# Edge gathers of a graph layer: an explicit bound on the row numbers of the indirect DMAs

## The chip, the cores and the metric

The kernel runs on one core of one Trainium2 chip. The metric is the device time in microseconds. Three runs of the kernel before took 1586.07, 1587.04 and 1588.51 us; the median is 1587.04 us.

## What is computed

A graph layer over 6250 nodes with 512 features and 106250 directed edges, sorted by their target, is followed by a mixture of 16 experts. Cut to what matters:

```python
def _L0_gnn_ref(x, src, dst, W_self, b_self, W_neigh, gamma, beta, alpha):
    deg = jax.ops.segment_sum(jnp.ones_like(src, dtype=x.dtype), dst, num_segments=N)
    inv_deg = 1.0 / jnp.maximum(deg, 1.0)
    agg = jax.ops.segment_sum(x[src], dst, num_segments=N)
    neigh = agg * inv_deg[:, None]
    h = x @ W_self + b_self + neigh @ W_neigh
    ...  # layer norm over features, gamma, beta, leaky slope alpha
    return h + x

x = x + _L0_gnn_ref(_layernorm(x), src, dst, ...)
x = x + _L0_ffn_ref(_layernorm(x)[None], gate_weight, w1, w2)[0]
```

The change touches `x[src]`, the fetch of one row per edge. `src` holds numbers from 0 to 6249.

## The kernel before

The work goes in three parts, one after another.

Projection. The rows of x are normalised in 49 tiles of 128 nodes and multiplied by W_neigh before they are aggregated. The product, split into a high and a low half of type float16, goes to a table in device memory (`table`, 6250 rows of 1024 float16 values, 2048 bytes a row, stored in line 427).

Edge stage. The 106250 edges are cut into 208 groups (`GROUPS`) of 4 times 128 edges (`GT` is 4). For each group GpSimd (POOL) issues four indirect DMAs in line 656; each fetches 128 rows of the table, one per partition, by a column of `idx_all`, into a ring of four group buffers (`GRING`, tile `gath`, printed as work). So there are 832 gathers of 256 KB. From the fifth group on, POOL first reads from a small table how many steps TensorE must have finished before the buffer is free (`value_load` in line 651), waits for that number on `c_step` (line 652) and executes a `nop` (line 653). The places behind the last edge of the last group get source number 0 (line 572 clears that part of the list) and target -1, so each number in `idx_all` is a row of the table.

TensorE (PE) takes the rows in 257 steps (`STEPS`): each step waits until its group has landed (`c_g`) and multiplies the rows by a 128 by 128 matrix of zeros and ones that ScalarE (ACT) builds (lines 781 and 787), so that the rows of one target are added up in PSUM (line 1035); line 1038 counts the edges, and its last matmul raises `c_step`. Beside the first 49 steps PE also computes x @ W_self for one tile a step (`side`, whose matmuls are in line 931). VectorE (DVE) finishes a tile of nodes when its last step is done (line 1411 is the first of its instructions). In the last 49 steps PE transposes the finished tiles (line 1052) and computes the gate's logits for them.

Experts. Then DVE and ACT sort the tokens by expert, and POOL gathers the tokens, 128 a time, in 114 indirect DMAs of line 715. PE multiplies them by the experts' weights, the means per expert are formed, and the result is mixed into the output. The gathers of line 715 wait for the list that DVE writes in line 1609.

Waits are written out by hand, each engine runs its program in order, and the only instructions that POOL executes between line 649 and line 658 are those named above.

Of the kernel before, what the change touches and what calls it, by code (L numbers as in the profile page):

```python
# [5 lines left out]
N, D, EXPERTS, FF = 6250, 512, 16, 256  # L6
# [13 lines left out]
GRING = 4  # L20
# [86 lines left out]
def build(nc, x, src, dst, w_self, b_self, w_neigh, gamma, beta, alpha, gate_t, w1_t, w2_t, out):  # L107
# [7 lines left out]
    with ctx:  # L115
# [3 lines left out]
        def sems(name, n):  # L119
            return [sem(f"{name}{i}") for i in range(n)]  # L120
# [68 lines left out]
        def cut(words, start=None):  # L189
            if start is not None:  # L190
                place[0] = start
            a = place[0]
            place[0] += words
            assert place[0] <= WORK, place[0]
            return work[:, a:a + words]
# [13 lines left out]
        idx_all = cut(GROUPS * GT, WORK - TABLES).bitcast(i32)  # L209
# [133 lines left out]
        c_g = sems("c_g", GRING)  # L343
# [225 lines left out]
        def _(pool):  # L569
# [79 lines left out]
            for g in range(GROUPS):  # L649
                if g >= GRING:  # L650
                    at = pool.value_load(finrow[0:1, g - GRING:g - GRING + 1], min_val=HOTS + 1, max_val=HOTS + STEPS)  # L651
                    pool.wait_ge(c_step, at)
                    pool.nop(nofuse=True)
                for w in range(GT):
                    t = GT * g + w
                    pool.indirect_dma_start(  # L656
                        out=gath[:, g % GRING, w, :], out_offset=None, in_=table[:, :],
                        in_offset=bass.IndirectOffsetOnAxis(ap=idx_all[:, t:t + 1], axis=0)).then_inc(c_g[g % GRING], 16)


            pool.wait_ge(d_zero, 16)
# [46 lines left out]
            for k in range(SLOTS):  # L708
                it, b = divmod(k, RING)
                if it:  # L710
# [6 lines left out]
                    in_offset=bass.IndirectOffsetOnAxis(ap=idx2[:, k:k + 1], axis=0)).then_inc(f_g[b], 16)  # L717
# [1001 lines left out]
```

## Time and profile before

| what | value |
|---|---|
| median of three runs | 1587.04 us |
| lowest, highest | 1586.07, 1588.51 us |
| span of the profiled execution | 1584.0 us |
| POOL busy | 986.1 us (62%) |
| gathers of line 656, busy | 793.9 us in 832 instructions |
| PE busy | 1149.7 us (73%) |
| DVE busy | 1079.2 us (68%) |
| ACT busy | 888.5 us (56%) |
| mean granted TensorE clock | 0.914 |

The page comes from one execution. Its span reaches from the first to the last instruction and is 3.0 us below the median of the runs. An instruction of an engine is shown with its busy time and with the idle time ahead of it, together with what ended that idle time; "issue" means that the engine waited for nothing which the profile shows. POOLq stands for POOL's sequencer, which fetches and issues instructions. The landing of a DMA is what releases the engines that wait for its data.

### The profile page before, as it was taken

Reading aid. Unit: us, or ns where it says so; the run is one execution under the profiler, and the core shown is the slowest. Engines: PE = TensorE matmul, PEld = TensorE weight load, DVE = VectorE, ACT = ScalarE, POOL = GpSimd, SP = SyncE. Lnnn points to the kernel's source line nnn. Section 1 sums busy time; section 2 is a strip of 40 time slices with the busy share of each in tenths; the row PEclk is TensorE's granted clock in tenths of the full one; section 3 lists DMA queues with packets and bytes.
Section 4 is the critical chain, followed back from the end, with each engine's and each line's share of the span. In section 5 each row is a group of like instructions: output and inputs, shape, how many; then the busy total and the mean of one; then the engine's idle time right before and its main releaser. Section 6 shows DMA issues by size and latency. Waiting matters only on the chain.

```text
span 1584.0 us, 36317 instructions
## 1 busy us (share of the span) xinstructions
PE 1149.7 (73%) x7603; PEld 615.1 (39%) x7604; DVE 1079.2 (68%) x2597; ACT 888.5 (56%) x1925; POOL 986.1 (62%) x1254
## 2 busy tenths in 40 slices
PE   4999999999655555665556555566667527999986
PEld 2555444444322222222222222224444315766741
DVE  5776236657667675777878778657666895677647
ACT  3565455555645444554444444437666696888850
POOL 5323377676777777777777777777777305676500
PEclk9999999999979898888898998979999958999995
DMA  5545378887888898899988888888887636777659
GB/s 186 162 157 172 125 219 269 260 250 248 273 273 274 260 268 240 256 300 299 298 289 288 295 293 295 265 247 250 248 253 235 226 130 186 243 238 243 201 172 334
DMA packets 140644, 384.92 MB, mean 243 GB/s; under 512 B 22358, under 2 KB 22488, under 8 KB 140524
## 3 DMA queue, kind: packets, MB, share of 16 engines
q0 software_dynamic: 76416, 250.05, 52.5%
q1 hardware_dynamic: 63580, 132.49, 23.3%
q10 hardware_dynamic: 528, 1.05, 0.2%
q8 instruction: 43, 0.70, 0.2%
q14 instruction: 77, 0.63, 0.1%
HBM read 323.78 MB, written 59.72 MB: 242 GB/s over the span
## 4 chain that ended last, share of the span: by engine, by line
PE 39%; POOL 26%; issue 18%; DVE 7%; DMA 6%; POOLq 2%; ACT 2%; DVEq 0%; SPq 0%; ACTq 0%
POOL work L656 25%; PE ps L931 13%; PE ps L1035 10%; PE ps L1127 6%; DMA work<-table,work 4%; PE ps L1138 3%; PE ps L1129 3%; POOLq L651 2%; PE ps L1205 1%; PE ps L979 1%; DMA work<-in_x 1%; DVE slots L1600 1%; ACT slots L846 1%; PE ps L1189 0%; DVE stats L1312 0%
## 5 line engine op out<-in xcount | busy, mean ns | idle before, releaser
L656 POOL DMA_INDIRECT work<-table,work x832 | 793.9, 954 | 284.8 <-issue 238.3
L1035 PE MATMUL ps<-work 128*128 x2056 | 552.9, 418 | 339.2 <-DMA work<-table,work 315.3
L1035 PEld LDWEIGHTS ps<-work 128*128 128x128 f16 x2056 | 212.4, 104 | 572.9 <-issue 421.3
L787 ACT ACTIVATE work<-work,ones 128x512 f16<-128x512 f16 x257 | 183.9, 716 | 300.8 <-PE ps L1038 300.7
L781 ACT ACTIVATE work<-iota_row,work 128x128 f16<-128x128 f32 x1028 | 327.5, 390 | 27.4 <-ACT work L787 23.9
L931 PE MATMUL ps<-wparts,slots 128*128 128x512 f16 x1176 | 271.9, 382 | 4.4 <-DVE work L1333 2.4
L715 POOL DMA_INDIRECT slots<-x_d,betab x114 | 110.4, 968 | 135.8 <-DVE betab L1609 67.3
L1411 DVE TENSOR_SCALAR inv<-ps 128x1 f32 (+2 forms) x49 | 7.7, 158 | 231.2 <-PE ps L1038 226.2
L931 PEld LDWEIGHTS ps<-wparts,slots 128*128 128x128 f16 x1176 | 112.4, 99 | 124.9 <-issue 7.3
L1127 PE MATMUL ps<-work,wparts 128*128 x456 | 155.7, 382 | 0.9 <-issue 0.4
L875 ACT COPY wparts<-ps 128x1024 f16<-128x1024 f16 x114 | 115.3, 1011 | 38.1 <-PE ps L1138 36.9
L1129 PE MATMUL ps<-work,wparts 128*128 x456 | 124.8, 274 | 0.0
L1636 DVE TENSOR_REDUCE work<-ps 128x256 f32<-128x512 f32 x114 | 78.4, 690 | 34.6 <-PE ps L1129 30.6
L1038 PEld LDWEIGHTS ps<-onesh,work 128*128 128x128 f16 x1028 | 66.9, 100 | 71.9 <-issue 19.8
L801 ACT COPY wparts<-ps 128x1024 f16<-128x1024 f16 (+1 forms) x49 | 49.4, 1008 | 79.3 <-PE ps L1052 79.3
L1628 DVE TENSOR_TENSOR slots<-slots,work 128x256 f32 x114 | 62.3, 546 | 35.9 <-issue 21.5
L793 ACT ACTIVATE slots<-ps,wscale 128x512 f32<-128x512 f32 (+1 forms) x49 | 33.6, 686 | 92.6 <-PE ps L931 92.6
L1138 PE MATMUL ps<-identh,slots 128*128 128x128 f16 x912 | 70.4, 221 | 7.2 <-DMA slots<-x_d,betab 7.2
L1138 PEld LDWEIGHTS ps<-identh,slots 128*128 128x128 f16 x912 | 61.0, 99 | 22.3 <-issue 7.4
L733 ACT ACTIVATE work<-work,gb,gs 128x512 f32<-128x512 f32 (+1 forms) x49 | 40.1, 821 | 45.4 <-POOL gb L624 45.3
L1038 PE MATMUL ps<-onesh,work 128*128 128x1 f16 x1028 | 63.5, 165 | 0.0
L869 ACT ACTIVATE work<-work,wscale 128x256 f32<-128x256 f32 x114 | 58.1, 510 | 8.8 <-DVE work L1636 8.1
(284 smaller groups left out, 1506.0 us busy)
## 6 DMA issues: line engine op xcount, KB each, us to landing
work<-in_x SPq DMA_DIRECT2D x96, 256.0 KB, 2.8
work<-in_w_t SPq DMA_DIRECT2D x48, 512.0 KB, 6.7
work<-table,work POOLq DMA_INDIRECT x832
table<-work SPq DMA_DIRECT2D x48, 256.0 KB, 2.0
x_d<-work SPq DMA_DIRECT2D x48, 256.0 KB
x_d<-slots SPq DMA_DIRECT2D x48, 256.0 KB
slots<-x_d SPq DMA_DIRECT2D x48, 256.0 KB
out_x<-slots SPq DMA_DIRECT2D x48, 256.0 KB
```

What stands on the lines that cost most here:

```text
L656: pool.indirect_dma_start(out=gath[:, g % GRING, w, :], out_offset=None, in_=table[:, :], in_offset=bass.IndirectOffsetOnAxis(ap=idx_all[: ...
L715: pool.indirect_dma_start(out=xf[:, b, :], out_offset=None, in_=x2_d[:, :], in_offset=bass.IndirectOffsetOnAxis(ap=idx2[:, k:k + 1], axis= ...
L781: last = act.activation(away[:, par, w, :], iota_row[:, :], ACT.Abs, bias=negd[:, ds(GT * k + w, 1)])
L787: act.activation(hot[:, slot, :, :], away[:, slot % 2, :, :], ACT.Relu, bias=ones[:, 0:1], scale=-1.0).then_inc(c_hot, 1)
L875: act.copy(xft[:, b, :, :, :], chunks16(bank16(6 + n % 2), P)).then_inc(f_xt, 1)
L931: last = pe.matmul(to, left(a, c), right(w, c), start=start and c == 0 and a == 0 and w == 0, stop=c == n - 1 and a == 1)
L1035: pe.matmul(ps[:, ds(bank, 1), :], hot[:, s, w, :], gath_row[:, ds(at + (2 * w + half) * D, D)].unsqueeze(1), start=False, stop=True, skip ...
L1038: last = pe.matmul(ps[:, BANKS:2 * BANKS, 0:1][:, ds(bank, 1), 0], hot[:, s, w, :], onesh[:, :], start=False, stop=True, skip_group_check= ...
L1127: pe.matmul(ps[:, HBANK + b, :].rearrange("p (u a n) -> p u a n", u=1, a=2), xft[:, b, 0, c, :], both, start=c == 0, stop=c == CHUNKS - 1, ...
L1129: last = pe.matmul(ps[:, HBANK + b, FF:2 * FF].unsqueeze(1), xft[:, b, 1, c, :], high, start=False, stop=c == CHUNKS - 1, skip_group_check ...
L1138: last = pe.transpose(bank16(6 + n % 2)[:, j * P:(j + 1) * P], xf[:, b, j * P:(j + 1) * P], identh[:, :])
L1636: dve.tensor_reduce(hid[:, b, :], ps[:, HBANK + b, :].rearrange("p (a n) -> p n a", a=2), X, ALU.add).then_inc(f_pre, 1)
```

## The change

Each of the 832 gathers of the edge stage is given `bounds_check=N - 1`, which is 6249, and `oob_is_err=False`: a row whose number is above the bound is skipped, and nothing is reported. Without the two arguments there is no bound, and `oob_is_err` has its default, True. The gathers of line 715 stay as they are.

```diff
                     t = GT * g + w
                     pool.indirect_dma_start(
                         out=gath[:, g % GRING, w, :], out_offset=None, in_=table[:, :],
-                        in_offset=bass.IndirectOffsetOnAxis(ap=idx_all[:, t:t + 1], axis=0)).then_inc(c_g[g % GRING], 16)
+                        in_offset=bass.IndirectOffsetOnAxis(ap=idx_all[:, t:t + 1], axis=0),
+                        bounds_check=N - 1, oob_is_err=False).then_inc(c_g[g % GRING], 16)
```

The program interface takes the bound as a number or as a register.

## Rows read from the trace of the kernel before

**Rows 1.** Page: span, and the chain that ended last by engine and line.

```profile
span 1584.0 us, 36317 instructions
...
PE 39%; POOL 26%; issue 18%; DVE 7%; DMA 6%; POOLq 2%; ACT 2%; DVEq 0%; SPq 0%; ACTq 0%
```

**Rows 2.** Windows by stage: stretch, length, each engine's busy us, clock, DMA share, GB/s.

```profile
core 0: us, PE busy (x) PEld busy (x) DVE busy (x) ACT busy (x) POOL busy (x), PEclk, DMA share, GB/s
190.60:1246.70 1056.10, 717.74 (x4512) 358.30 (x4511) 721.31 (x1886) 568.41 (x1378) 793.86 (x832) 0.92 0.84 266
```

**Rows 3.** The gathers of line 656: durations, and idle time ahead of them.

```profile
L656 POOL DMA_INDIRECT work<-table,work x832: 942/949/1379, 190.6 to 1245.7; - x167
...
  issue: 238.3, 781
  PE ps L1038: 24.0, 50
```

**Rows 4.** Timeline of POOL, one group of gathers and the next one's first: start, duration, idle time before.

```profile
607.64 0.94 POOL L656 DMA_INDIRECT work<-table,work  x1 [0.30 <-PE ps L1038]
...
611.39 0.96 POOL L656 DMA_INDIRECT work<-table,work  x1 [0.30 <-issue]
612.66 0.95 POOL L656 DMA_INDIRECT work<-table,work  x1 [0.30 <-issue]
```

**Rows 5.** Windows of the edge stage's beginning, middle and end, columns as in rows 2.

```profile
190.60:405.40 214.80, 210.07 (x1136) 97.62 (x1134) 118.16 (x312) 122.15 (x300) 156.08 (x164) 1.00 0.81 253
405.40:1041.00 635.60, 368.44 (x1880) 173.78 (x1881) 465.56 (x1198) 314.24 (x793) 481.50 (x506) 0.87 0.87 278
1041.00:1246.80 205.80, 139.32 (x1499) 86.92 (x1498) 137.69 (x377) 132.13 (x286) 156.28 (x163) 0.96 0.80 245
```

**Rows 6.** Timeline of POOL, gathers that waited over 0.5 us for a buffer.

```profile
292.60 0.95 POOL L656 DMA_INDIRECT work<-table,work  x1 [1.56 <-PE ps L1038]
...
314.68 0.95 POOL L656 DMA_INDIRECT work<-table,work  x1 [2.35 <-PE ps L1038]
...
385.35 0.95 POOL L656 DMA_INDIRECT work<-table,work  x1 [2.34 <-PE ps L1038]
```

**Rows 7.** POOL's sequencer at lines 651 and 653: min, median and max ns.

```profile
L651 POOLq TENSOR_LOAD <-work x204: 283/289/1005, 195.8 to 1229.7; - x102
L651 POOLq FUSED_REGOPS  x204: 147/147/193, 196.3 to 1230.0; - x102
L651 POOLq SEQ_ASSERT  x204: 18/18/32, 196.5 to 1230.2; - x102
L653 POOLq EVENT_SEMAPHORE  x204: 17/17/17, 202.5 to 1236.0; - x102
```

**Rows 8.** The chain of waits about 605 us: start, us, what.

```profile
604.92 0.60 POOLq L651
```

**Rows 9.** Page: all packets; POOL's DMA queue: packets, MB, share of 16 engines.

```profile
DMA packets 140644, 384.92 MB, mean 243 GB/s; under 512 B 22358, under 2 KB 22488, under 8 KB 140524
...
q0 software_dynamic: 76416, 250.05, 52.5%
```

**Rows 10.** The waits: who waited for whom, us in total, times, longest.

```profile
PE ps L1035 <- DMA work<-table,work: 315.3, 166, 5.8
ACT work L787 <- PE ps L1038: 300.7, 138, 7.3
DVE inv L1411 <- PE ps L1038: 226.2, 43, 33.4
```

**Rows 11.** The token gathers of line 715, durations as in rows 3.

```profile
L715 POOL DMA_INDIRECT slots<-x_d,betab x114: 941/948/1192, 1314.0 to 1510.4; - x114
```

**Rows 12.** Groups of POOL: a tensor instruction on four elements a partition.

```profile
L614 POOL TENSOR_TENSOR fix<-guess 128x4 f32<-128x4 f32 x39 | 7.8, 200 | 3.1
```

**Rows 13.** Timeline at the stage's end: the last gathers, and DVE behind PE.

```profile
1240.05 0.16 DVE L1411 TENSOR_SCALAR inv<-ps 128x1 f32<-128x1 f32 x1 [0.77 <-PE ps L1038]
...
1245.73 0.95 POOL L656 DMA_INDIRECT work<-table,work  x1 [0.30 <-issue]
```

## The prediction

> **What bounds the kernel now.** I read the page's chain first. PE has 39% of it, POOL 26%, and 18% is "issue", time in which an engine waited for nothing that the profile shows [rows 1]. Shares of a whole span hide which stage an edit touches, so the windows by stage come next: the gathers of line 656 fill the stretch from 190.6 to 1246.7 us, 1056.1 of the 1584.0 us, and POOL does nothing else there [rows 2]. Then the gathers themselves. Nearly all take 949 ns (median, 942 at least), and the idle time ahead of them is 238.3 us of issue in 781 gaps, which makes 0.305 us a gap, plus 24.0 us for PE in 50 [rows 3]. The timeline shows what that looks like: a gather starts each 1.25 us, with 0.30 us between two, at a group's first gather as at its others [rows 4]. 832 times 1.25 us is 1040 us, all but 16 us of the stage. So the stage runs at the pace of POOL's own work, and the reader should see in rows 4 that the 0.30 us is part of that pace and no wait.
>
> The windows inside the stage correct this in one place. Up to 405.4 us PE is busy for 210.07 of 214.80 us: there it also has the W_self product, and it is PE that sets the pace. After that it is busy for 368.44 of 635.60 and 139.32 of 205.80 us [rows 5]. POOL's real waits say the same: five gathers waited between 1.56 and 2.35 us for a buffer, the first at 292.6 and the last at 385.35 us, 10.3 us together with the usual gap of 0.30 in each, hence 8.8 us of real slack [rows 6]. 164 gathers lie ahead of 405.4 us and 506 and 163 (one of them counted in both) behind it, 668 in all [rows 5]. Downstream everybody waits for them: PE 315.3 us for landings, ACT 300.7 us for PE, DVE 226.2 us for PE [rows 10]. Even at the end DVE's last chain is set off by a PE step, at 1240.05 us, while the last gathers are still issued [rows 13].
>
> **The exchange rate.** It follows that x ns more per gather cost 668x behind 405.4 us, and nothing ahead of it until 164x exceeds 8.8 us, that is until x is 53. So 10 ns are 6.7 us. What a measurement of this kernel can tell from no change is about 0.2%, 3.2 us, and that is 4.8 ns per gather. A gain of x ns would bring the same 668x, until the next limit: the 16 DMA engines are busy for 87% of the middle [rows 5], so at most 13% of 841 us, 109 us.
>
> **The change part by part.** (1) Rows saved. None: each number in the list is a row of the table, since the unused places hold number 0. The bytes and the descriptors stay, so the landings and the 87% stay. Cost 0, and no gain. This has one answer as long as the bound is counted in rows.
>
> (2) Handing over the bound. A number has to reach the instruction as an operand. If a register is set once, it costs nothing; if it is set ahead of each gather, there are 832 more instructions on POOL's sequencer. Rows 7 have the neighbours of such an instruction: 17 to 18 ns for the simplest, 147 ns for a fused register operation. What covers them: in front of each group the sequencer already executes a load, a register operation and an assertion, 289 + 147 + 18 = 454 ns, and then the wait and the nop, and the gap of the group's first gather stays 0.30 us like the others' [rows 4, 7]. The chain shows line 651 at 604.92 us for 0.60 us, and the gather it belongs to starts at 607.64 us [rows 4, 8]: the sequencer is 2.1 us ahead, more than one gather. Four times 147 ns are 588 ns a group, beside 5.01 us in which POOL works off four gathers; the lead would still be made. I take 0. Were the cover gone, because an operand that comes from a register cannot be queued ahead, it would cost 18 to 147 ns per gather: 668 times that is 12 to 98 us, and at the upper end the first 164 gathers add 164 x 0.147 - 8.8 = 15 us, which makes 113 us.
>
> (3) Comparing the row numbers. The queue of these transfers is named software_dynamic [rows 9] and each gather costs POOL 949 ns, so I assume that the comparison is made where POOL writes the descriptors, on its own path. No gather with a bound stands in the trace; the token gathers have none either and take the same, 948 ns [rows 11]. From below: the compare is already there with some bound that lets everything pass, and costs 0; or the default form does a check with its error report that the new form leaves out, a gain. A gain is priced by the cheapest check in the trace, the sequencer's assertion with 18 ns [rows 7]: 668 x 0.018 = 12 us. From above: a separate pass of POOL over 128 numbers, priced by its smallest tensor instructions, 200 ns [rows 12]: 668 x 0.200 = 134 us, and 24 us more from the first stretch. Between them lies a compare and branch inside the loop: a row now costs 949 / 128 = 7.4 ns for reading its number, working out an address and writing the descriptors; a compare at a twentieth to a sixth of that is 0.4 to 1.2 ns a row, 50 to 160 ns a gather, 33 to 120 us (estimates from rows 3). I take 0, because the nearest rows, 832 and 114 gathers of different tables, agree to 1 ns and so look like one fixed piece of work done on all 128 numbers, into which a compare fits without a step of its own; but this is a choice, not a reading, and both ends stay in the range.
>
> (4) Packets. The queue carries 250.05 MB in 76416 packets [rows 9]. 22358 packets of all queues are under 512 B [rows 9]; if 16 of them belong to each of the 946 gathers, 15136 in all, 61280 packets of 4080 bytes remain, two rows each (an estimate from rows 9). A bound might force one row per packet, since a row could be missing. The price would fall on the DMA engines, which have 13% left [rows 5]; q0 uses 52.5% of the span for its 250 MB. I take 0: up to 13% longer transfers are hidden by the issue pace, and beyond that it would show as a DMA share near 1.
>
> Sum against the profiled execution: 1584.0 + 0 + 0 + 0 + 0 = 1584.0 us of span, and 3.0 us around it by the median of the runs: 1587.0 us.
>
> The rows show that writing descriptors is the pace of the stage: 0.95 of each 1.25 us [rows 4]. The Trainium skill, "DMA: Bandwidth & Descriptors", section "Anatomy of one DMA — SWDGE (gpsimd) path", calls descriptor generation "small, variable" and says that the fixed cost of some 2 us is mostly the receipt of the last write. Taken literally this would make any check free, and the time 1587.0 us by another road; the gaps of rows 4 speak against it, for nothing hides behind a landing there. By the rows a check of 50 ns costs 33 us, by the page nothing.
>
> **The rivals.** *The check costs in the descriptor loop* (slower). One mechanism: each of the 128 numbers meets a compare and a branch, the duration of line 656 rises from 949 ns by 5 to 200 ns, and from 4.8 ns on it can be told. For it: POOL's work is on the path, with no slack for 668 gathers. Against it: the sameness of all gathers. At 60 ns: 668 x 0.060 = 40 us, plus 164 x 0.060 - 8.8 = 1 us: 1628 us. Chance 0.34.
>
> *The register is on the path* (slower). The duration stays, the gap of 0.30 us grows by 18 to 147 ns. Against it speaks the lead of 2.1 us [rows 4, 8]. At 18 ns 1599 us, at 147 ns 1700 us. Chance 0.08, nearer to the lower end.
>
> *The default form was the dearer one* (faster). The duration falls, because no error has to be looked for; 18 ns give 1575 us. For it speaks only that something must happen today with a number outside the table. Chance 0.12, of which 0.03 for more than 18 ns.
>
> *The change does not do what it says*: if the bound is compared in another unit than rows, rows are skipped, the DMA share falls and the result lacks rows. The issue pace would hardly move; chance 0.02, and its time would be that of one of the other cases.
>
> *No effect*: chance 0.44, 1587.0 us, own range 1584 to 1590 us.
>
> **How the numbers follow.** The likeliest case gives 1587.0 us. Slower by over 0.2%: 0.34 + 0.08 = 0.42. Faster by over 0.2%: 0.12, and 0.01 of the case of the wrong unit: 0.13. Within 0.2%: 0.45. The range takes in the gain of 18 ns, 1575 us, with a little beyond, 1574; upward it follows the loop's check to 110 ns: 668 x 0.110 = 73 us, plus 164 x 0.110 - 8.8 = 9 us, which is 1670; I take 1668. Left out are about 0.04 below and 0.12 above.
>
> **What would show it.** The median duration of line 656 decides (3), the usual gap of 0.30 us decides (2), the packets of q0 and the DMA share decide (4). If POOL's pace is 1.25 us again, the span must be 1584 within its scatter. If it is not, the five waits of rows 6 should shrink first, and the length behind 405.4 us should grow by 668 times the difference. I am wrong if the pace moves by more than 4.8 ns, or if the span moves while the pace does not.

## The result, and the profile after

The changed kernel took 1623.98 us (median of 4 runs, 1622.89 to 1625.09) against 1587.77 us for the kernel before beside it. The ratio is 1.0224, with a 95% interval from 1.0211 to 1.0238: 2.2% slower. The profiled execution's span grew from 1584.0 to 1621.5 us, by 37.5 us. The forecast of no change was wrong. The time lies in the range, and it came where the first rival had put it: in the gather's own duration. That rival's mechanism, a compare for each of the 128 numbers, is another matter (see the gathers of fewer rows).

The page and the gathers' line after the change. The durations are min, median and max ns, then come first and last start:

```profile
span 1621.5 us, 37149 instructions
...
DMA packets 140651, 384.98 MB, mean 237 GB/s; under 512 B 22358, under 2 KB 22488, under 8 KB 140524
...
q0 software_dynamic: 76416, 250.05, 51.7%
```

```profile
L656 POOLq MOVE  x832: 29/29/35, 190.2 to 1273.4; - x167
L656 POOL DMA_INDIRECT work<-table,work x832: 994/999/1297, 191.0 to 1281.8; - x167
...
  issue: 240.1, 788
  DMA table<-work: 23.2, 1
  PE ps L1039: 14.9, 43
```

Against [rows 3] the median has risen from 949 to 999 ns, and even the shortest gather takes 994 instead of 942. A second line is new: 832 register moves of 29 ns on POOL's sequencer, one ahead of each gather, which are exactly the 832 instructions that the page counts more. POOL's queue carries the packets and MB of [rows 9], to the packet; over all queues there are 7 packets more, all on the queue q14, whose kind the page calls instruction. (Lines below 656 have moved down by one: 1039 here is 1038 before.)

The timeline of POOL, the stretch of [rows 4]:

```profile
606.30 1.00 POOL L656 DMA_INDIRECT work<-table,work  x1 [0.30 <-issue]
607.61 0.99 POOL L656 DMA_INDIRECT work<-table,work  x1 [0.30 <-issue]
608.91 1.00 POOL L656 DMA_INDIRECT work<-table,work  x1 [0.30 <-issue]
610.21 1.00 POOL L656 DMA_INDIRECT work<-table,work  x1 [0.30 <-issue]
```

The gap is 0.30 us as before, the gather is longer, and the pace is 1.30 instead of 1.25 us.

Where the 37.5 us lie: the first gather starts 0.5 us later (191.04 for 190.57). From the first start to the last, the stage takes 1281.82 - 191.04 = 1090.8 us, where it took 1245.73 - 190.57 = 1055.2: 35.6 more. Behind the last start come 339.7 instead of 338.3 us, 1.4 more. The 35.6 us come out of two sums. The gathers are busy for 836.8 instead of 793.9 us, 42.9 more, and the idle time ahead of them, without the first gather's, is 240.1 + 14.9 = 255.0 instead of 262.3 us, 7.3 less. What shrank are the waits for a buffer in the first stretch. Five waits of over 0.5 us stood there, all of over 1.5 us [rows 6]; two of over 0.5 us are left:

```profile
364.80 1.00 POOL L656 DMA_INDIRECT work<-table,work  x1 [1.17 <-PE ps L1039]
...
386.88 1.00 POOL L656 DMA_INDIRECT work<-table,work  x1 [1.25 <-PE ps L1039]
```

The 165th gather, the first behind the stretch in which PE sets the pace, divides the stage. Before (first line) and after (second):

```profile
405.52 0.94 POOL L656 DMA_INDIRECT work<-table,work  x1 [0.44 <-issue]
407.90 1.00 POOL L656 DMA_INDIRECT work<-table,work  x1 [0.30 <-issue]
```

From the first gather to this one it takes 216.9 instead of 214.9 us, 1.9 more, and from this one to the last 873.9 instead of 840.2 us, 33.7 more.

The windows, with the columns of [rows 2], answer to [rows 5]:

```profile
190.60:405.40 214.80, 209.50 (x1130) 97.27 (x1129) 116.68 (x308) 120.55 (x297) 163.19 (x163) 1.00 0.81 249
405.40:1041.00 635.60, 378.55 (x1809) 173.31 (x1808) 449.59 (x1156) 304.30 (x767) 487.81 (x486) 0.82 0.85 268
```

Up to 405.4 us PE is as busy as before and nearly as many gathers start, 163 for 164. In the middle only 486 gathers start where 506 did. The DMA share fell from 0.87 to 0.85, so the DMA engines had less to do and not more. PE's granted clock fell too (0.87 to 0.82) and its matmuls took longer, but it waited for landings 318.2 us in all (315.3 before), and behind 386.88 us no gather waited over 0.5 us for it, so it was not what the stage waited for.

### The profile page after: what moved, and what is told of

Its sections match the earlier page's. It is cut to its first block, busy times and chain, and to the rows that moved or that the text cites. A ratio compares the mean times of both kernels' runs of the same rounds, so it can differ in the third digit from the quotient of the medians.

```text
span 1621.5 us, 37149 instructions
## 1 busy us (share of the span) xinstructions
PE 1184.8 (73%) x7603; PEld 626.2 (39%) x7604; DVE 1078.1 (66%) x2597; ACT 889.0 (55%) x1925; POOL 1028.6 (63%) x1254
## 2 busy tenths in 40 slices
DMA packets 140651, 384.98 MB, mean 237 GB/s; under 512 B 22358, under 2 KB 22488, under 8 KB 140524
## 3 DMA queue, kind: packets, MB, share of 16 engines
q0 software_dynamic: 76416, 250.05, 51.7%
## 4 chain that ended last, share of the span: by engine, by line
PE 40%; issue 25%; POOL 18%; DVE 5%; DMA 4%; POOLq 4%; ACT 2%; DVEq 0%; SPq 0%; ACTq 0%
POOL work L656 17%; PE ps L932 13%; PE ps L1036 12%; PE ps L1128 6%; POOLq L651 3%; DMA work<-table,work 3%; PE ps L1139 3%; PE ps L1130 3%; PE ps L1206 1%; PE ps L980 1%; DMA work<-in_x 1%; POOLq L656 1%; DVE slots L1601 1%; ACT slots L847 1%; PE ps L1039 0%
## 5 line engine op out<-in xcount | busy, mean ns | idle before, releaser
L656 POOL DMA_INDIRECT work<-table,work x832 | 836.8, 1006 | 278.2 <-issue 240.1
L1036 PE MATMUL ps<-work 128*128 x2056 | 585.8, 437 | 340.8 <-DMA work<-table,work 318.2
L1036 PEld LDWEIGHTS ps<-work 128*128 128x128 f16 x2056 | 218.4, 107 | 591.4 <-issue 451.8
L1637 DVE TENSOR_REDUCE work<-ps 128x256 f32<-128x512 f32 x114 | 78.3, 690 | 35.5 <-PE ps L1130 31.4
L1039 PEld LDWEIGHTS ps<-onesh,work 128*128 128x128 f16 x1028 | 69.5, 103 | 79.7 <-issue 33.7
```

The source lines that it names most:

```text
L656: pool.indirect_dma_start(out=gath[:, g % GRING, w, :], out_offset=None, in_=table[:, :], in_offset=bass.IndirectOffsetOnAxis(ap=idx_all[: ...
L1036: pe.matmul(ps[:, ds(bank, 1), :], hot[:, s, w, :], gath_row[:, ds(at + (2 * w + half) * D, D)].unsqueeze(1), start=False, stop=True, skip ...
L1039: last = pe.matmul(ps[:, BANKS:2 * BANKS, 0:1][:, ds(bank, 1), 0], hot[:, s, w, :], onesh[:, :], start=False, stop=True, skip_group_check= ...
L1637: dve.tensor_reduce(hid[:, b, :], ps[:, HBANK + b, :].rearrange("p (a n) -> p n a", a=2), X, ALU.add).then_inc(f_pre, 1)
```

## The experiments

The theory after the result: a bound makes each indirect DMA dearer by 50 ns of POOL's own work, whatever it is told to do with rows beyond it, and this shows in the time where POOL sets the pace and nowhere else. The rivals: the silent skipping is what costs (B); the register move or its hand-over costs (C); and, for the size of the price, that it goes by the rows compared (E) and not by the instruction (D).

**The bound, with an error for rows beyond it**

```diff
-                        bounds_check=N - 1, oob_is_err=False).then_inc(c_g[g % GRING], 16)
+                        bounds_check=N - 1).then_inc(c_g[g % GRING], 16)
```

> The bound stays on all 832 gathers, but a row beyond it is reported (oob_is_err left at True). Theory A, the comparison itself costs: the median of the gathers is 999 ns as in the changed kernel, ratio to the kernel before 1.022. Theory B, skipping without an error is what costs: the median is back near 949 ns and the ratio is 1.000 to 1.003. In between would mean both.

Measured: ratio 1.028, interval 1.0259 to 1.0301, and

```profile
L656 POOL DMA_INDIRECT work<-table,work x832: 1006/1012/1525, 190.6 to 1290.7; - x167
```

B falls: with the error form the price is 63 ns, 13 more than in the silent one, where medians of the same form differ by up to 4 ns from kernel to kernel (946 and 949 without a bound, 998 to 1002 with the silent one). A held in kind, and was low in size. The exchange rate fits: 668 x 0.063 + (164 x 0.063 - 8.8) = 43.6 us, measured 0.028 x 1588.6 = 44.5.

**The silent form, without a bound**

```diff
-                        in_offset=bass.IndirectOffsetOnAxis(ap=idx_all[:, t:t + 1], axis=0)).then_inc(c_g[g % GRING], 16)
+                        in_offset=bass.IndirectOffsetOnAxis(ap=idx_all[:, t:t + 1], axis=0),
+                        oob_is_err=False).then_inc(c_g[g % GRING], 16)
```

(The edit is shown against the kernel before.)

> Only the other argument: oob_is_err=False with no bound. Theory A (the bound costs): 949 ns, ratio 1.000. Theory B (the silent form costs): 999 ns, ratio 1.022. If the default form looked for errors at a price, as my rival of the faster side had it, the median would fall below 949 ns.

Measured: ratio 0.9993, interval 0.9983 to 1.0002, and

```profile
L656 POOL DMA_INDIRECT work<-table,work x832: 940/946/1348, 192.5 to 1247.0; - x167
```

The two arguments taken apart give the split: without a bound, the silent form costs nothing, and the price is the bound's. The 3 ns below [rows 3] are no gain: kernels whose gathers were not touched, or only the first 164 of them, show 946 as well (below). So the default form without a bound pays nothing that could be saved, and my rival of the faster side falls.

**The bound in a register that is set once**

```diff
+            top_row = nc.alloc_register(pool.engine, "top_row")
+            pool.reg_mov(top_row, N - 1)
             for g in range(GROUPS):
...
-                        bounds_check=N - 1, oob_is_err=False).then_inc(c_g[g % GRING], 16)
+                        bounds_check=top_row, oob_is_err=False).then_inc(c_g[g % GRING], 16)
```

> The bound is put into a register once, ahead of the loop, so the 832 register moves of 29 ns on POOL's sequencer are gone and all else is as in the changed kernel. Theory A (the cost sits in the gather's own work, the moves are covered): gathers stay at 999 ns, gaps at 0.30 us, ratio 1.022 like the changed kernel, within 0.2% of it. Theory C (the move or its hand-over costs): 832 times 29 ns, up to 24 us, come back, ratio near 1.007.

Measured: 1622.10 us, ratio 1.0206, interval 1.0189 to 1.0223, beside the changed kernel's 1.0211 to 1.0238. The moves are gone from the sequencer, and the gathers (first fence) and their gaps in the timeline (second) are as they were; line 658 is line 656 here:

```profile
L658 POOL DMA_INDIRECT work<-table,work x832: 996/1002/1281, 191.2 to 1282.0; - x167
```

```profile
600.37 1.00 POOL L658 DMA_INDIRECT work<-table,work  x1 [0.31 <-issue]
601.68 1.00 POOL L658 DMA_INDIRECT work<-table,work  x1 [0.30 <-PE ps L1041]
```

C falls. Of the 24 us of moves nothing measurable came back: the medians differ by 1.9 us, the two intervals overlap, and theory C wanted a ratio near 1.007. As a way out of the price this edit is worth nothing that these runs can tell.

**The bound on the first 164 gathers, and on the other 668**

```diff
+                    bound = dict(bounds_check=N - 1, oob_is_err=False) if g < 41 else {}
                     pool.indirect_dma_start(
                         out=gath[:, g % GRING, w, :], out_offset=None, in_=table[:, :],
-                        in_offset=bass.IndirectOffsetOnAxis(ap=idx_all[:, t:t + 1], axis=0)).then_inc(c_g[g % GRING], 16)
+                        in_offset=bass.IndirectOffsetOnAxis(ap=idx_all[:, t:t + 1], axis=0), **bound).then_inc(c_g[g % GRING], 16)
```

This too is against the kernel before. The second kernel has `g >= 41`.

> The bound on the first 41 groups alone, 164 gathers, the stretch in which TensorE sets the pace. By the exchange rate of the prediction their 164 x 0.050 = 8.2 us fit into the 8.8 us of slack: ratio 1.000, under 1.002. If there is no such slack, 8.2 us: ratio 1.005.

Measured: ratio 1.0005, interval 0.9994 to 1.0015. POOL's line, and from its timeline two of the three waits of over 0.5 us that are left where [rows 6] had five:

```profile
L657 POOL DMA_INDIRECT work<-table,work x832: 942/946/1338, 190.6 to 1246.3; - x167
```

```profile
364.49 0.99 POOL L657 DMA_INDIRECT work<-table,work  x1 [1.55 <-PE ps L1039]
386.57 1.00 POOL L657 DMA_INDIRECT work<-table,work  x1 [1.56 <-PE ps L1039]
```

The last gather starts at 1246.3 us for 1245.7, so of some 8 us of extra work 0.6 reached the last gather. (At the 165th gather the delay was 2.0 us; the rest of the stage then took 838.7 us for 840.2, which is the difference between single executions.)

> The bound on groups 41 to 207 alone, 668 gathers, none of them with cover. By the exchange rate 668 x 0.050 = 33 us, ratio 1.021; with the changed kernel's ratio of 1.0224 this leaves under 4 us for the first 164. If the time simply went by the number of gathers, it would be 37.5 x 668 / 832 = 30 us, ratio 1.019.

Measured: ratio 1.0198, interval 1.0168 to 1.0227. Both numbers of the expectation, 1.021 and 1.019, lie in that interval, so this run alone does not tell a share by position from a share by count. The pair does: by count the first 164 would be worth 37.5 x 164 / 832 = 7.4 us, a ratio of 1.0047, and the interval of the first kernel ends at 1.0015. In the second the five waits stand as before (1.66, 2.40, 1.80, 2.26 and 2.33 us). Its 165th gather, the first with a bound, is this:

```profile
406.63 1.02 POOL L657 DMA_INDIRECT work<-table,work  x1 [0.38 <-issue]
```

The last starts at 1278.4 us, 871.8 us later, where it took 840.2: 31.6 us, which is the measured 0.0198 x 1588.3 = 31.4 us. Behind the 164th gather the price is paid whole, and no slack pays for it.

**Fewer rows in a gather**

In two kernels each group has four kinds of gather: 128 rows without and with the bound, and 64 (or 32) rows without and with it. The rows that are not fetched are left out of the result, and the buffers are cleared once ahead of the loop. The last of the four kinds, with 64 rows:

```diff
+                    out_w = gath[:, g % GRING, w, :]
+                    at_w = idx_all[:, t:t + 1]
...
+                    if w == 3:
+                        pool.indirect_dma_start(
+                            out=out_w[0:64, :], out_offset=None, in_=table[:, :],
+                            in_offset=bass.IndirectOffsetOnAxis(ap=at_w[0:64, :], axis=0),
+                            bounds_check=N - 1, oob_is_err=False).then_inc(c_g[g % GRING], 16)
```

> Each group has one gather of 128 rows without a bound, one of 128 with it, one of 64 rows without, one of 64 with; the other 64 rows are left out and hold zeros or old rows. Theory D, a fixed price per instruction: both pairs differ by 50 ns. Theory E, a price per row: the pair of 128 differs by 50, the pair of 64 by 25 ns. The time of the kernel says nothing here, as half the rows of two gathers in four are missing.

The lines of the table's gathers, in that order:

```profile
L660 POOL DMA_INDIRECT work<-table,work x208: 947/952/1233, 206.2 to 1263.4; - x104
L664 POOL DMA_INDIRECT work<-table,work x208: 1008/1012/1244, 207.6 to 1264.6; - x104
L669 POOL DMA_INDIRECT work<-table,work x208: 906/910/1242, 209.0 to 1265.9; - x104
L673 POOL DMA_INDIRECT work<-table,work x208: 944/948/1228, 210.2 to 1267.2; - x104
```

> As the kernel with 64 rows, with 32 rows in the short gathers. Theory D (fixed): the short pair differs by 50 ns. Theory E (per row): by 12 ns. Together with 128 and 64 rows the three points give a line, price = fixed part + part per row.

The two gathers of 32 rows, without and with the bound:

```profile
L669 POOL DMA_INDIRECT work<-table,work x208: 873/877/1170, 206.7 to 1256.5; - x104
L673 POOL DMA_INDIRECT work<-table,work x208: 932/937/1242, 207.9 to 1257.7; - x104
```

The price is 60 ns at 128 rows (in both kernels), 38 at 64, 60 at 32. That is on no line, and the medians of the pair of 128 rows differ by 60 where they differ by 50 when all gathers are alike. The place in the group (first to fourth) is not the reason: in the changed kernel the median is 999 ns at each of the four places. The means of the pair say less of it (965 and 1015 ns in one kernel, 963 and 1019 in the other, 954 and 1006 with all alike), so an effect of the mixing of some 10 ns is in the medians alone. Hence two more kernels, cleared in the same way, in which all 832 gathers have 64 rows:

```diff
-                        out=gath[:, g % GRING, w, :], out_offset=None, in_=table[:, :],
-                        in_offset=bass.IndirectOffsetOnAxis(ap=idx_all[:, t:t + 1], axis=0)).then_inc(c_g[g % GRING], 16)
+                        out=gath[0:64, g % GRING, w, :], out_offset=None, in_=table[:, :],
+                        in_offset=bass.IndirectOffsetOnAxis(ap=idx_all[0:64, t:t + 1], axis=0)).then_inc(c_g[g % GRING], 16)
```

> All 832 gathers fetch 64 rows and none has a bound; the other half of each group is left out and holds zeros (the buffers are cleared once). The mixed kernel showed 910 ns for such a gather. If the duration depends only on the instruction and not on its neighbour, the median is 910 ns here too, and POOL's pace is 1.21 us.

> The same with the bound on all 832 gathers of 64 rows; half the rows are left out. Against the kernel with 64 rows and no bound: a fixed price per instruction gives 50 ns more, as with 128 rows; a price per row gives 25 ns; the mixed kernel showed 38. This pair has no mixed neighbours and decides between them.

Without and with the bound:

```profile
L657 POOL DMA_INDIRECT work<-table,work x832: 897/903/1404, 203.9 to 1230.3; - x167
```

```profile
L657 POOL DMA_INDIRECT work<-table,work x832: 937/942/1351, 207.0 to 1257.2; - x167
```

39 ns at 64 rows, 50 at 128. The expected 50 (D) and 25 (E) were both missed. A price in proportion to the rows is out: in the mixed kernels a quarter of the rows costs as much as all of them. A price that is exactly fixed is out as well, by 39 against 50. What stands is a price of 38 to 60 ns that does not follow the rows; why 64 rows are the cheapest case isn't known, and the 32 rows were seen between other gathers only. The two kernels of 64 rows, one run each, took 1575.2 and 1597.2 us, 22.0 us apart.

The same lines size the gather itself. 64 rows more cost 949 - 903 = 46 ns, 0.7 ns a row, and 128 rows at that rate are 92 ns: by this estimate some 860 of the 949 ns come with the instruction and not with its rows. From 64 to 32 rows the mixed kernels give 910 - 877 = 33 ns, 1.0 ns a row, so the straight line is a rough one.

**Rows that are skipped**

```diff
+            ln.link(pool.memset(gath_row[:, :], 0.0))
...
-                        bounds_check=N - 1, oob_is_err=False).then_inc(c_g[g % GRING], 16)
+                        bounds_check=N // 2 - 1, oob_is_err=False).then_inc(c_g[g % GRING], 16)
```

A second kernel has the bound 0. Both leave out the rows beyond their bound, and both start the stage some 15 us later, for the clearing.

> The bound is half the table, 3124, so about half of the rows are skipped and their places keep old rows; the buffers are cleared once ahead of the loop. If the bound is counted in rows, the queue's MB fall from 250 to about 140 and the DMA share of the edge stage from 0.84 to about 0.5. Theory F, a skipped row still costs POOL its comparison and its descriptors: gathers stay near 999 ns and the stage's length stays. Theory G, a skipped row saves its descriptors, at up to (949 / 128) 7.4 ns a row: gathers fall to 999 - 64 x 7.4 = 525 ns at the least, and the stage shrinks until TensorE sets its pace.

The gathers, and from the page the packets and POOL's queue:

```profile
L657 POOL DMA_INDIRECT work<-table,work x832: 992/998/1279, 206.7 to 1295.1; - x167
```

```profile
DMA packets 140651, 275.78 MB, mean 169 GB/s; under 512 B 35865, under 2 KB 35995, under 8 KB 140524
...
q0 software_dynamic: 76416, 140.86, 30.5%
```

> The bound is 0, so all rows but those with number 0 are skipped. With half the rows skipped the gathers took 998 ns and the number of packets stayed, so a skipped row is handled like a fetched one: again 998 ns, the same 76416 packets, about 33 MB on the queue, and a DMA share of the edge stage near 0.2. If a skipped row were cheaper or dearer for POOL, it shows here at double size.

The same two views:

```profile
L657 POOL DMA_INDIRECT work<-table,work x832: 992/998/1286, 205.6 to 1295.3; - x167
```

```profile
DMA packets 140644, 167.77 MB, mean 103 GB/s; under 512 B 75470, under 2 KB 75600, under 8 KB 140524
...
q0 software_dynamic: 76416, 32.90, 8.7%
```

The bound counts rows: half the table leaves 140.86 MB, and the bound 0 leaves 32.90. F holds and G falls. Skipped or fetched, a row costs POOL the same. The number of packets stays 76416, while with half the table 13507 more of them are under 512 bytes than in the changed kernel, and with the bound 0 75470 - 22358 = 53112 more. The gathers' rows travel two to a packet: 832 x 64 = 53248 packets of 4096 bytes. In the traces' records of the single packets, one with both its rows skipped has 8 bytes (13507 and 53112 packets) and one with one row skipped 2052 (26408 packets with half the table), so a skipped row leaves 4 bytes, and its packet is still sent. The stage takes 1088.4 and 1089.7 us, as in the changed kernel (1090.8), though the DMA share behind 405 us has fallen to 0.53 and 0.21. The transfers were not what the stage waited for. Nor was PE's clock: behind 405 us, up to 1280 us, it was 0.88 with the bound 0 and 0.84 in the changed kernel, at the same length of the stage.

**The bound on the token gathers instead**

```diff
-                    in_offset=bass.IndirectOffsetOnAxis(ap=idx2[:, k:k + 1], axis=0)).then_inc(f_g[b], 16)
+                    in_offset=bass.IndirectOffsetOnAxis(ap=idx2[:, k:k + 1], axis=0),
+                    bounds_check=N, oob_is_err=False).then_inc(f_g[b], 16)
```

> The edge gathers as before, the bound (6250, the last row of that table) on the 114 token gathers of line 715 instead. The instruction should be 50 ns dearer there as well, 5.7 us of work. POOL waits for TensorE 54.4 us in 72 of them, so by the reading that only a gather on the path costs time the ratio is 1.000, under 1.001; if POOL's time counted wherever it stands, 1.0036.

Measured: ratio 0.9994, interval 0.9984 to 1.0004. The edge gathers, untouched, and the token gathers with their bound:

```profile
L656 POOL DMA_INDIRECT work<-table,work x832: 941/946/1344, 192.3 to 1246.6; - x167
```

```profile
L715 POOL DMA_INDIRECT slots<-x_d,betab x114: 994/1007/1243, 1316.2 to 1513.0; - x114
```

The median rises from 948 [rows 11] to 1007 ns, 59 ns, on a gather of another table, and the time does not move. 114 x 0.059 = 6.7 us, a ratio of 1.0042, lies outside the interval. The idle time ahead of these gathers, now and (below) before:

```profile
  issue: 40.9, 86
  PE ps L1139: 11.1, 17
```

```profile
  PE ps L1138: 54.4, 72
  issue: 9.7, 30
```

Their busy time grew by 8.9 us (110.4 to 119.3), these two kinds of idle time shrank together by 12.1 us (64.1 to 52.0), and from the first start to the last it takes 196.8 for 196.4 us: where POOL waits for PE, the price is paid out of the wait. Most of what is left is now put down to "issue"; that the register move between the wait and the gather does this is likely and not shown.

## Why the prediction was wrong, point by point

**The stage's bound and the exchange rate were right.** The prediction had 668x behind 405.4 us and nothing ahead of it up to 53 ns. With the measured 50 ns that is 33.4 us, and from the 165th gather to the last 33.7 were measured. The other 3.8 of the 37.5 us: the first gather started 0.5 us later, 1.4 us came behind the last one (that part lies between 337.0 and 342.7 us in the traces of the other kernels, so this is scatter), and 1.9 us came in the first stretch, which the prediction had at nothing. POOL's busy time on the first 164 gathers, before and after (stretch, length, busy us, clock, DMA share, GB/s):

```profile
190.50:405.50 215.00, 156.10 (x164) 1.00 0.81 253
191.00:407.80 216.80, 165.07 (x164) 1.00 0.81 251
```

They had 9.0 us more work, and the slack that they found was not the whole 8.8 us: the two waits that are left hold 1.17 + 1.25 - 2 x 0.30 = 1.8 us of it, so 7.0 were used. The slack is there, as described, but not to the last microsecond; the bound on the first 164 gathers alone costs no measurable time.

**Part (1), no rows saved,** was right, and stronger than stated: even when nearly all rows are skipped, the stage gets no shorter.

**Part (2), the register,** was right in both halves. The instruction exists (29 ns, between the 18 and 147 ns that I had set as bounds), and it is covered: the gap stays 0.30 us.

**Part (3) is the step that failed.** I took 0 because all gathers last the same and a comparison would therefore fit into a fixed piece of work. The sameness was read correctly, the conclusion was not. The work is indeed nearly fixed, 860 of 949 ns, but that says nothing about whether a further piece fits in for free: another piece of 38 to 60 ns, which does not follow the rows, is added to it. So the term was put at 0 ns a gather, and it measured 50: 33.7 us behind the 165th gather. The compare in the loop, the mechanism of the first rival, was sized by a wrong picture too. 949 / 128 = 7.4 ns is no price of a row; a row costs 0.7 ns, and a comparison at "a twentieth to a sixth" of 7.4 ns came near 50 ns by luck. The ends that came from rows were a pass of its own on POOL, 200 ns, and 0, and no row spoke for the lower one. With the operation absent from the trace, on an engine without slack, 0 was the end least supported, and the rival with 0.34 should have been the forecast.

**Part (4), the packets,** was right: their number did not change with the bound, nor with skipped rows, and there are two rows in each (4096 bytes, where the estimate had 4080).

**The rule weighed there.** The measured rows settle it: 39 to 63 ns more on all 832 gathers came back as 22 to 45 us of span or device time, at DMA shares between 0.60 and 0.85. The Trainium skill, "DMA: Bandwidth & Descriptors", section "Anatomy of one DMA — SWDGE (gpsimd) path", puts most of a DMA's fixed cost into the receipt of its last write. The trace does not speak against it: the token gathers before the change landed 3.9 us (median) after their start, of which POOL's own 0.95 us is a quarter. But a stage that issues 832 gathers in a row pays that quarter each time. The Trainium skill, "Perfetto Trace Analysis", section "DMA Instruction — SWDGE (GPSIMD)", says that the recorded end of such an instruction is the writing of its last descriptor; the trace agrees, in that the price stands in the busy time and not in the gap of 0.30 us.

What stays open is what inside the instruction takes the 50 ns, and why 64 rows pay less than 32. No run here looks inside it.

## What to carry to other kernels

Find the engine whose pace a stage keeps, and count instructions there: an option on an instruction that is issued 832 times back to back is paid 668 times over here, while the same option on 114 instructions that wait for another engine came free. Price an operand that the trace doesn't show by experiment, and where none can be run, don't price it by zero because the instruction looks uniform: the bounds here were 0 and 200 ns, and it was 50. In a stage like this one, give an indirect DMA a bound only where indices can lie beyond it, and don't expect that skipped rows make it faster.

## What the runs showed of the hardware that I had not expected

An indirect DMA of 128 rows of 2048 bytes costs POOL 949 ns, of 64 rows 903 and of 32 rows (between others) 877 ns: the rows are nearly free for POOL. Reporting is dearer than silence, 1012 against 999 ns, though no row was ever beyond the bound. A skipped row keeps its place in a packet, with 4 bytes: 76416 packets with 250.05, 140.86 or 32.90 MB in them. And between gathers of other kinds a bounded gather of 128 rows had a median of 1012 instead of 999 ns; whether the gather ahead does that no run isolates.
